# Four ring banks in PSUM instead of three and one: the attention outputs join the ring, and every engine gets a new order

## What is computed

```
x = x + att0                            # cross-attention L0 (16 heads); only its first sequence is added, to all
x = x + mamba(rms(x))                   # L1: in_proj, conv of 4 taps, silu, decay pairs, gate, out_proj
x = x + attention1(ln(x), ctx) @ Wo     # L1: 8 heads of 32
x = ln(x + attention2(x, x))            # L2: 16 heads of 16, causal, keys cut to a length
x = ln(x + attention3(x, ctx))          # L2: 16 heads, masked queries
x = ln(x + fc2(relu(fc1(x))))           # L2
x = ln(x + attention4(x, ctx, causal))  # L3: 16 heads
x = x + down(gelu(up(x)))               # L3: 256 -> 1024 -> 256
```

## Time and profile before

| what | value |
|---|---|
| time, median of 3 runs | 1795.92 us (1793.83 to 1796.07) |
| time of the profiled execution | 1793.13 us |
| its span, first to last instruction | 1791.1 us |
| PE busy | 1684.8 us, 94% of the span |
| DVE, ACT, POOL busy | 1345.6, 1368.2, 549.9 us |
| granted TensorE clock, mean over the span | 0.978 |
| the chain that ended last | PE 78%, DVE 14%, ACT 3%, issue 3%, POOL 2% |

### The profile page before, as it was taken

One profiled execution on the slowest core, in us unless ns is written; L12 is line 12 of the kernel. 1 busy time (PEld: TensorE's weight loads), 2 busy tenths in 40 slices (PEclk: granted clock), 3 DMA queues, 4 the chain that ended last, 5 costly groups with the idle time before them and its releaser, 6 DMA issues.

```text
span 1791.1 us, 54559 instructions
## 1 busy us (share of the span) xinstructions
PE 1684.8 (94%) x21072; PEld 1437.7 (80%) x21072; DVE 1345.6 (75%) x3355; ACT 1368.2 (76%) x4026; POOL 549.9 (31%) x1288
## 2 busy tenths in 40 slices
PE   5679999999999999999999999999999999999876
PEld 4467888888888888888888888888888888888765
DVE  3477788877777888778788877778888778878542
ACT  2267887887888788788878877887888788778763
POOL 1233233332333333233333333323333233333110
PEclk7799999999999999999999999999999999999988
DMA  7000000000000000000000000000000000000000
GB/s 257 7 7 8 8 2 11 11 11 11 11 2 11 11 11 11 11 11 2 11 11 11 11 11 11 2 11 11 11 11 10 11 2 11 11 8 5 5 4 9
DMA packets 26174, 26.89 MB, mean 15 GB/s; under 512 B 2240, under 2 KB 25024, under 8 KB 25792
## 3 DMA queue, kind: packets, MB, share of 16 engines
q1 hardware_dynamic: 25920, 23.41, 4.0%
HBM read 19.21 MB, written 4.19 MB: 13 GB/s over the span
## 4 chain that ended last, share of the span: by engine, by line
PE 78%; DVE 14%; ACT 3%; issue 3%; POOL 2%; DVEq 0%; DMA 0%; SPq 0%; POOLq 0%; ACTq 0%
PE ring L626 21%; PE ring L620 20%; PE ring L614 17%; PE output L718 5%; PE score L676 5%; DVE conv L1274 4%; PE ring L795 3%; PE ring L805 2%; ACT exps L992 2%; PE output L708 2%; POOL stat L1437 1%; DVE tz L1312 1%; DVE res L1170 1%; DVE bn L1157 1%; DVE res L1358 1%
## 5 line engine op out<-in xcount | busy, mean ns | idle before, releaser
L992 ACT ACTIVATE exps<-score,neg_max 128x128 f32<-128x128 f32 x1808 | 495.0, 412 | 73.3 <-DVE neg_max L1181 70.5
L1181 DVE TENSOR_REDUCE neg_max<-score 128x4 f32<-128x512 f32 x452 | 286.4, 681 | 76.5 <-PE score L676 74.4
L1437 POOL TENSOR_TENSOR stat<-stat 128x1 f32<-128x1 f32 x224 | 129.3, 577 | 530.7 <-DVE stat L1153 529.8
L998 ACT COPY weights<-ring 128x512 f32<-128x512 f32 x452 | 244.0, 604 | 57.2 <-PE ring L614 55.5
L614 PE MATMUL ring<-const,exps 128*128 128x128 f32 x1808 | 248.7, 279 | 24.2 <-ACT exps L992 10.4
L614 PEld LDWEIGHTS ring<-const,exps 128*128 128x128 f32 x1808 | 198.4, 142 | 60.1 <-issue 27.7
L1268 DVE SCALAR_TENSOR_TENSOR conv<-raw,vectors,conv 128x128 f32<-128x128 f32 x576 | 168.4, 348 | 6.8
L620 PE MATMUL ring<-actT,w_q 128*128 128x128 f32 x1024 | 142.5, 282 | 0.5 <-ACT actT L964 0.5
L620 PEld LDWEIGHTS ring<-actT,w_q 128*128 128x128 f32 x1024 | 127.3, 192 | 10.9 <-issue 6.3
L964 ACT COPY actT<-ring 128x256 f32<-128x256 f32 x224 | 81.9, 378 | 70.7 <-PE ring L614 70.6
L676 PE MATMUL score<-K,QB 32*128 32x128 f32 x3616 | 134.9, 283 | 0.1
(11 more groups left out here) (163 smaller groups left out, 3531.2 us busy)
## 6 DMA issues: line engine op xcount, KB each, us to landing
cT<-in_ctxT SPq DMA_DIRECT2D x32, 128.0 KB, 2.2
x_in<-in_x SPq DMA_DIRECT2D x32, 128.0 KB, 2.1
out<-result SPq DMA_DIRECT2D x32, 128.0 KB, 1.7
row_all<-in_rows SPq DMA_DIRECT2D x1, 1420.0 KB, 10.0
w_in<-in_in_proj SPq DMA_DIRECT2D x1, 1288.0 KB, 7.3
w_k<-in_k SPq DMA_DIRECT2D x4, 256.0 KB, 5.8
w_v<-in_v SPq DMA_DIRECT2D x4, 256.0 KB, 5.9
w_q<-in_q SPq DMA_DIRECT2D x4, 256.0 KB, 6.5
```

The source lines that it names most:

```text
L992: last = run(exps[:, n, h * P:(h + 1) * P], of, ACT.Exp, bias=neg_max[:, m, h:h + 1])
L998: nc.scalar.copy(weights[:, buffer(it, a_, l, t, WEIGHT_BUFFERS), half * 4 * P:(half + 1) * 4 * P], t_[:, :]).then_inc(read, 1)
L1181: nc.vector.tensor_reduce(neg_max[:, m, 4 * half:4 * half + 4].rearrange("p (b h) -> p b h", b=each), score[:, first:first + each, 0:4 // ...
L1437: tt(stat[:, l, 10:11], stat[:, l, 2:3], stat[:, l, 4:5], ALU.pow).then_inc(S[done], 1)
```

## The change

`RING_BANKS` goes from 3 to 4, the bank `output` goes, and the `values` tasks become ring jobs (`NO_RING` no longer names them). PE claims the bank in `values` instead of waiting for `output_read`; `finish1` and `out_turned` read the ring bank and free it through `bank_read`; the fourth of the four row semaphores becomes the bank's own. So a ring job now waits for the reader of the job four before it, and the `values` tasks count among the jobs: 62 of them for each sequence. `evacuated_all` gets a `then`, to leave out a wait that the claim makes anyway. No arithmetic is changed or moved between engines.

```diff
 TASKS = dict(
-    loadx=-19.632, loadc=-0.373, x1=-12.582, x1r=18.202, xhat=40.805, xhatT=6.043, dt=11.125, softplus=10.471, am=-3.466,
...
+    loadx=-39.297, loadc=-21.957, x1=-31.388, x1r=0.609, xhat=34.036, xhatT=-8.817, dt=1.27, softplus=-2.884, am=-12.308,
+    xbc0=-7.003, xbc1=-5.859, z1=-5.461, z0=1.147, K1=-7.656, V1=-0.645, conv0=10.153, conv1=1.914, silu=8.942, pairs=2.154,
...
-RING_BANKS = 3
+RING_BANKS = 4
...
-NO_RING += [f"{task}{a_}" for task in ("quads", "values", "attT") for a_ in PARTS]
+NO_RING += [f"{task}{a_}" for task in ("quads", "attT") for a_ in PARTS]
...
-        output = pb("output", [P, 512])
...
-            def evacuated_all(it, *jobs):
+            def evacuated_all(it, *jobs, then=None):
 
                 last = {job(it, *j)[0]: j for j in sorted(jobs, key=lambda j: place(it, *j))}
                 for j in last.values():
-                    evacuated(it, *j)
+                    evacuated(it, *j, then)
...
             def values(it, a_, l):
 
-                if a_:
-                    pe.wait_ge(S["output_read"], nth_output(it, a_, l) - 1)
+                output, full = claim(it, f"values{a_}", l)
...
-                                    last.then_inc(S[f"att_full{r}"], 1)
+                                    last.then_inc(full if r == TILES - 1 else S[f"att_full{r}"], 1)
...
             def back(it, a_, l):
-                pe.wait_ge(S["output_read"], nth_output(it, a_, l))
+                evacuated(it, f"values{a_}", l, back_job(a_, l))
...
             def Wo(it, l):
-                pe.wait_ge(S["output_read"], nth_output(it, 1, l))
+                evacuated(it, "values1", l, ("Wo", l))
...
             def out_turned(it, a_, l):
-                for r in range(TILES):
+                for r in range(TILES - 1):
                     act.wait_ge(S[f"att_full{r}"], nth_output(it, a_, l))
-                nc.scalar.copy(attT[:, att_buffer(it, a_, l), :], output[:, :]).then_inc(S["output_read"], 1)
+                t, read = filled(it, f"values{a_}", l)
+                nc.scalar.copy(attT[:, att_buffer(it, a_, l), :], t[:, :]).then_inc(read, 1)
...
                 def finish1(l):
 
-                    for r in range(TILES):
+                    for r in range(TILES - 1):
                         dve.wait_ge(S[f"att_full{r}"], nth_output(it, 1, l))
-                    step(nc.vector.reciprocal(rec1[:, :], output[:, D:]))
-                    tt(actT[:, l, :, :].rearrange("p c k -> p (c k)"), output[:, 0:D], rec1[:, :],
-                       ALU.mult).then_inc(S["output_read"], 1)
+                    t, read = filled(it, "values1", l)
+                    step(nc.vector.reciprocal(rec1[:, :], t[:, D:]))
+                    tt(actT[:, l, :, :].rearrange("p c k -> p (c k)"), t[:, 0:D], rec1[:, :], ALU.mult).then_inc(read, 1)
```

More of the change, by code:

```diff
@@ L55 @@
[L55 to L58, removed]
@@ new lines @@
+    e3=26.002, n3=26.41, finish3=21.372, norm3=36.468, x4T=29.166, fc1=31.148, fc2=31.994, norm4=36.026, K4=31.657, V4=32.925,
+    x5T=32.94, Q4=33.558, finish4=46.075, norm5=40.873, x6T=41.8, up0=42.154, up1=42.297, down=68.294, store=78.752, quads1=9.708,
+    scores1_0=10.704, turn1_0=11.473, values1=12.06, quads2=15.325, scores2_0=16.842, scores2_1=17.864, turn2_0=18.34,
+    turn2_1=18.516, values2=19.823, attT2=22.328, back2=21.152, quads3=25.921, scores3_0=25.992, scores3_1=26.33, turn3_0=26.863,
@@ new lines @@
+SETUP = dict(
+    Q0=-132.818, K0=-130.2751, V0=-129.8, quads0=-129.0547, scores0_0=-128.5909, turn0_0=-128.326, scores0_1=-127.1157,
+    turn0_1=-127, values0=-126.0869, attT0=-125.4926, back0=-124.7552, prep_in=-125.2505, finish0=-123.8643, prep_masks=-123.7236,
+    prep_out=-123.6283, bias=-126.0551, prep_q1=-122.7999, load_mamba=-145.4515, load_w1=-139.1362, load_w2=-137.8872,
+    load_w3=-136.0581)
+SHIFT = dict(ACT=dict( x1=19.18048, xhatT=0.47389, softplus=-1.78934, xbc0=0.08721, z0=0.93507, V1=0.28049, silu=-7.42736, pairs=0.89048, ld=0.15489,
+                   Y=1.20935, uT=0.278, xnT=-0.59829, Q1=0.03827, x2T=-0.43961, K2=0.59511, Q2=0.59286, V2=0.00092, x3T=0.21483, row=-0.04211,
+                   Q3=-0.03488, V3=0.58681, x4T=0.96954, fc1=0.11166, K4=-0.25599, x5T=0.33078, Q4=0.29048, x6T=0.20394, up0=1.0231, up1=1.27684,
+                   turn1_0=0.43258, attT2=-2.3464, turn3_0=-0.25935, turn3_1=-0.19474, attT3=2.86684, turn4_0=-0.08028, turn4_1=0.08661,
+                   attT4=1.95409),
+             DVE=dict( x1=18.96859, x1r=-12.46257, xhat=-42.37766, softplus=0.76516, K1=1.52212, conv0=-12.34117, conv1=-1.89334, silu=-6.49255,
+                   pairs=0.7517, ld=0.61333, decayed=-0.07487, Y=0.66363, uT=0.92596, proj=0.52368, finish1=2.17189, Wo=0.43298, e2=1.20634,
+                   n2=1.16124, finish2=-1.45382, norm2=2.96979, x3T=-0.62876, K3=1.41344, n3=0.26465, finish3=8.03121, norm3=-6.42493,
+                   fc2=0.50192, norm4=-2.62733, V4=0.88733, Q4=-0.07898, finish4=-5.11165, norm5=0.81823, down=0.45604),
+             POOL=dict( x1r=-11.26888, dt=-8.88759, softplus=-0.53932, am=10.06185, z1=6.59717, z0=2.15891, uT=0.61107, proj=-0.07643, Q2=2.80685,
+                   n2=3.61778, finish2=-3.55958, Q3=-1.2856, n3=0.79695, finish3=8.93534, fc2=-0.2655, V4=-1.08309, finish4=-4.52039,
+                   norm5=3.41211),
+             SP=dict( loadx=-3.2709, loadc=-0.98266, store=0.13316))
```

230 lines of the change are left out of this document (82 added, 148 removed).

## The result

The changed kernel takes 1739.66 us, the median of 4 runs (1739.34 to 1740.16), beside 1795.41 us of the kernel before on the same chip: the ratio is 0.9691, with a 95% interval of 0.9674 to 0.9708. The profiled span is 1737.6 us, 53.5 less than before.

The account below looks back on a forecast made before the run. PE's work and waits per period, plus two edges, bound the kernel. Terms -1.46 + 0.45 + 0.10 = -0.9, taken as -0.8 with crumbs, times 27 periods: -22, so 1774 us; forecast 1765 to 1783, wider range 1754 to 1802.

Parts of the forecast that it names:

- five stalls: PE waits at `pairs`, `turn2_0`, `up0`/`up1`, `x4T` and `x2T`: all taken as gone, -1.46 us a period.
- ACT's stretch: ACT's work between `quads4` and `values4`: PE would wait 0.9 us there, 0.45 of it new in each period.
- the edges: Filling and emptying of the pipeline at start and end: taken as 0, of -5 to +5 us.
- The rest is crumbs under 0.2 us.: PE's excess beyond the 1.46 us traced, out of 2.3 us a period: small waits, not costed one by one.
- `norm4`, +0.10: On DVE behind `Y`'s two multiplies: it would end just after PE reaches `x5T`, costing 0.1 us a period.
- `silu` down to 0.95: DVE's multiply ahead of `pairs`: falls from 2.65 to 0.95 us once `am`, with L1483, moves some 10 us ahead.
- rival 3: POOL's gate of `z0` starts before `silu`; PE waits 1.35 us more every period: 1811 us, chance 0.12.
- Full relief: First rival: nothing new is late and ACT's stretch is hidden, -1.46 us in 27 periods: 1757 us, chance 0.18.
- rival 2: New tight places, such as `e2` to `n2`, take everything back: 1788 to 1799 us; chance 0.18 with no effect.
- DVE's loop: Fifth rival: a loop through DVE keeps the period at 52.06 us: 1796 us; chance 0.18 together with tight places.

Follow-up runs that it names:

- the best kernel here: The changed kernel with the `silu` multiply moved ahead of `nonzero` on DVE from the second sequence on: 1737.53 us, and 1736.0 us when run again.
- e1: The changed code with four ring banks, but the order tables of the kernel before: 1770.31 us, ratio 0.9864 to the kernel before.
- e6: The changed kernel, with ACT copying `V3` out of PSUM in four instructions instead of one: 1740.18 us.
- e7: The changed kernel, with `z1` of the first sequence alone put back ahead of `xbc0`, and so also ahead of `K1`: 1743.84 us.
- e4: The changed kernel, with `am` moved back on POOL to its old place behind `Q2`: 1743.98 us, ratio 0.9714 to the kernel before.
- e2: The kernel before, with three ring banks and `output`, given all five new order tables: 1828.2 us, ratio 1.0183 to the kernel before.
- e3: The kernel before, with `am` run straight behind `softplus` on POOL from the second sequence on: 1817.27 us, ratio 1.0121 to the kernel before.
- e8: The changed code with the order tables of before and three ring banks, the `values` tasks being ring jobs: 1919.39 us, ratio 1.0697 to the kernel before.
- e9: The changed kernel with `silu` ahead of `nonzero` on DVE and, for the first sequence, `K1` behind `xbc1`: 1740.84 us.

## Why the prediction was wrong

The sign was right, and so was the mechanism of the bank: claims that waited for a reader. The terms of the sum were mis-sized. The five stalls gave less than I took; the small ones that I put at nothing, ACT's stretch that I put at +0.45, and the edges outweighed that and made the change more than twice as good as forecast.

1. **The five stalls, -1.46.** `turn2_0` gave 0.34 of 0.41, `up` 0.21 of 0.23, `x2T` 0.15 of 0.25, `pairs` 0.14 (0.49 to 0.35 in the table, where I had taken 0.42), and `x4T` nothing of 0.15: it takes 0.37 in both kernels, and 0.31 in the best kernel here, so at most 0.06 of it shows as a stall. Together 0.84, little more than half of what I took.
2. **"The rest is crumbs under 0.2 us."** This step failed. `ld` to `fc2` was 0.26 too long and `turn1_0` to `values4` 0.20, and the bank alone (e1) removes both but for 0.03. With a deeper ring a wait vanishes wherever a claim was late, also where no bracket shows. Smaller distances gave another 0.14, net of new ones (the largest, 0.16, is behind `V4`). I had counted the 2.3 us of excess and then costed 1.46 of it.
3. **ACT's stretch, +0.45, and `norm4`, +0.10.** Neither came. From the end of `quads4` ACT needed 0.9 us to the first exps and 11.35 to the last of `turn4_1`'s weights (810.19 to 821.54), 12.2 in all, where I had 12.8 to 13.4; PE came for them at 821.94. But the place was rightly named: e6 added 0.44 us of ACT there and PE lost 0.27. A chain estimated 5 to 10% too long turned 0.4 us of slack into a stall.
4. **Edges, 0 of -5 to +5.** They gave -7.3 and -3.8. I read `z1` behind `xbc` as a loss of up to 3 us through the dt chain; but PE waited 7 us for the conv and 1 us for the decays, so the conv was the longer chain, and `xbc` first shortens it (e7: 2.6 us from `xhatT` to `xbc0` lost). The early `am`, which I had put no edge value on, is another 3.3 us (e4). Counted from the first `xhatT`, the first `down` comes after 246.0 us before and 236.0 after the change; 2.6 are lost ahead of `xhatT` (30.4 and 33.1), which no term of mine had. The deeper ring alone (e1) takes 247.0 for this, the new order alone (e2) 250.1; only together do they gain. The end of the kernel is 3.8 us shorter at a granted clock of 0.884 behind the `down` of sequence 28 instead of 0.837, and e4 lost 2.8 us there at a lower clock with the order unchanged; what moves the clock there I didn't test.
5. **`silu` down to 0.95 by `am` going away.** Half right. The multiply fell to 1.35, since the gate of `z0` took L1483's place beside it. That is rival 3: its race did happen, POOL came first by 0.07 us, but it cost 0.4 us and not the whole length of the gate. That `am` would be harmless in its new place was luck of the new order: in the old one (e3) it cost 22 us.
7. **Rivals 1, 2 and 5.** Full relief gave 1757; the truth is past it, by points 2 and 4. No tight place of rival 2 showed a wait. DVE's loop doesn't set the period.

In numbers: 28 periods at -1.51, that is -42.4 us where I had -22, make 20 us of the 31 missed, the edges 11.

Of what the changed profile was to show, the `down` distance (51.2 to 51.4) and the median of L1225 were wrong, a wait of `pairs` stayed, `values4` didn't wait; no wait of `turn2_1`, and 32 and 31 loads, were right.

## What to carry to other kernels

A deeper ring removes waits in every place where a claim was late, most of them too short to be listed: sum the distances from task to task, and cost all of the excess, not the part that has a name. A wait of PE can cost more than its length: in e8 the granted clock fell behind it. A bank and an order have to be judged together: here the order alone lost 33 us and the bank alone won 25, less than half of what both win. An instruction moved out of one collision has to be followed on the other engine's timeline to where it lands, and so has what moves up behind it.

## What the runs showed of the hardware

- DVE and POOL held each other up by degrees. L1483 on POOL, two inputs, started 0.13 us before the multiply: it took 2.65 us instead of 0.95. L1427, one input and a constant, started 0.07 us before it: the multiply took 1.36, and the gate its usual 1.51, though both ran at once for 1.3 us. With DVE first by 0.16 us (e6) the multiply took 0.95, and the gate 2.15. The Trainium skill, "SBUF — State Buffer", section "Who interferes with whom", says that the first to issue blocks the other for its whole length: so it was in the first and nearly in the third case, not in the second. Nor in e3's second collision: DVE's L1181 began 0.05 us ahead of POOL's L1520, and it was DVE's that took 1.06 us instead of 0.53. The starts of these pairs lie 0.05 to 0.16 us apart in the trace, so which of two was issued first is not shown beyond doubt.
- In e8 PE sat idle for 2.26 us ahead of `down`, at a granted clock of 1.00. Over the 5.5 us of work behind that the clock had a mean of 0.69, so part of it ran at 1.2 GHz, and 16 matmuls took 5.38 us instead of 3.70.
- 0.44 us more work on ACT left the time unchanged within 1 us, as it decided that race the other way.
- At the start, TensorE ran at 1.2 GHz from 33 to 36 us in both kernels. With `K1` right behind the transpose, and PE busy without a gap, the granted clock was 0.96 in the next 3 us; with 0.51 us idle ahead of `xbc0` (e9) it was still 0.50, and 24 matmuls took 5.29 us instead of 3.32.
